# Masks moved into key rows, exps by bank, another merged order, one load of the spread queries, and a new start, in an eight-batch chain of four attentions

## The reference, cut to what matters

```
x = L0(x, ctx)        # 16 heads of 64, 256 positions, projections from x and ctx, layer norm
x = L1(ctx, x)        # 16 heads of 16, keys from [ctx, x] (256), key mask, MLP
x = L2(x, ctx)        # 16 heads of 16, 128 keys, key mask, MLP
x = L3(x, ctx)        # 16 heads of 8, 256 queries, 256 keys, key mask:
    attn = where(kv_mask, q @ k * scale, -inf); softmax
    mean = attn @ v; ex2 = attn @ (v * v); std = sqrt(relu(ex2 - mean**2))
    out  = (instance_norm(x) * std + mean) * mask
```

## Time and profile before

| | |
|---|---|
| median of three runs | 1008.47 us |
| the profiled execution, its own time | 1012.25 us |
| its span in the profile | 1010.5 us |
| TensorE busy (matmul) | 935.5 us, 93% of the span |
| VectorE busy | 559.5 us, 55% |
| ScalarE busy | 456.2 us, 45% |
| GpSimd busy | 292.4 us, 29% |
| DMA traffic | 86.54 MB, mean 86 GB/s |

### The profile page before, as it was taken

How to read it: one execution, slowest core, us unless ns; L and a number is a source line. 1 busy time by engine, 2 the same in 40 slices (tenths; PEclk the granted TensorE clock), 3 DMA queues, 4 the chain that set the end, 5 groups by cost and what they waited for, 6 DMA issues and landing times.

```text
span 1010.5 us, 21161 instructions
## 1 busy us (share of the span) xinstructions
PE 935.5 (93%) x8450; PEld 596.5 (59%) x8450; DVE 559.5 (55%) x890; ACT 456.2 (45%) x795; POOL 292.4 (29%) x402
## 2 busy tenths in 40 slices
PE   6989989999999998999999999999999999898995
PEld 5555764666647665567646666466665675455552
DVE  4344467445664557555675456644576546664554
ACT  2423444445444544445544454345544454442424
POOL 5230222334212432115322242124321243222401
PEclk9999999999999999999999999999999999999999
DMA  9500324113140132303241130401414031310220
GB/s 362 190 38 2 125 75 146 38 43 136 36 156 19 57 139 81 108 6 126 79 146 38 43 134 32 154 28 43 141 50 143 14 120 44 119 53 2 98 55 6
DMA packets 36728, 86.54 MB, mean 86 GB/s; under 512 B 8472, under 2 KB 26008, under 8 KB 28824
## 3 DMA queue, kind: packets, MB, share of 16 engines
q1 hardware_dynamic: 36632, 85.18, 24.5%
HBM read 77.24 MB, written 7.86 MB: 84 GB/s over the span
## 4 chain that ended last, share of the span: by engine, by line
PE 67%; DVE 12%; issue 6%; DMA 5%; ACT 5%; SPq 4%; POOL 1%; DVEq 0%; ACTq 0%; POOLq 0%
PE GP L1107 6%; PE GP L1118 6%; PE GP L660 6%; DVE nm L1592 5%; PE GP L662 5%; PE PV L821 4%; PE GP L1091 4%; PE PV L860 3%; PE GP L900 3%; PE SC L883 3%; PE PV L1031 3%; DMA Qx<-q_parts 2%; PE GP L667 2%; PE SC L1018 2%; PE SC L804 2%
## 5 line engine op out<-in xcount | busy, mean ns | idle before, releaser
L1592 DVE TENSOR_REDUCE nm<-MX 128x4 bf16<-128x1024 f32 (+1 forms) x168 | 206.4, 1229 | 125.3 <-PE MX L751 48.3
L1363 ACT ACTIVATE Pr<-SC 128x1024 f32<-128x1024 f32 x120 | 122.7, 1023 | 153.6 <-PE SC L883 76.9
L1966 POOL TENSOR_TENSOR Psum<-Pr 128x512 f32<-128x512 f32 x64 | 81.5, 1274 | 163.4 <-ACT Pr L1363 163.4
L660 PE MATMUL GP<-zP,W 128*128 128x128 f32 x512 | 106.3, 290 | 7.7 <-DMA W<-w 7.7
L662 PE MATMUL GP<-uP,W 128*128 128x128 f32 x512 | 99.7, 277 | 0.0
L660 PEld LDWEIGHTS GP<-zP,W 128*128 128x128 f32 x512 | 78.3, 193 | 29.0 <-issue 27.3
L1392 ACT ACTIVATE Pr<-SC,bcol 128x512 f32<-128x512 f32 x96 | 60.8, 685 | 51.3 <-PE SC L1018 50.7
L1934 POOL TENSOR_TENSOR stat<-stat,half 128x1 f32<-128x1 f32 x24 | 13.7, 570 | 224.4 <-DVE stat L1800 171.2
L662 PEld LDWEIGHTS GP<-uP,W 128*128 128x128 f32 x512 | 78.5, 194 | 0.0
L821 PE MATMUL PV<-Pr,V 128*64 128x256 f32 x512 | 70.8, 398 | 0.0
L1118 PE MATMUL GP<-WB,work 128*128 128x256 f32 x256 | 60.8, 386 | 6.5 <-DVE work L1731 6.4
(11 more groups left out here) (221 smaller groups left out, 1750.3 us busy)
## 6 DMA issues: line engine op xcount, KB each, us to landing
W<-w SPq DMA_DIRECT2D x20, 1024.0 KB, 5.3
WA<-w1a SPq DMA_DIRECT2D x8, 1024.0 KB, 7.2
WB<-w1b SPq DMA_DIRECT2D x8, 1024.0 KB, 9.5
WA<-w2a SPq DMA_DIRECT2D x8, 1024.0 KB, 4.8
WB<-w2b SPq DMA_DIRECT2D x8, 1024.0 KB, 7.0
Kx<-k_parts SPq DMA_DIRECT2D x24, 192.0 KB
Qx<-q_parts SPq DMA_DIRECT2D x24, 192.0 KB
scratch<-U SPq DMA_DIRECT2D x14, 256.0 KB, 2.0
```

The source lines that it names most:

```text
L660: pe.matmul(dst, W0[:, piece, 2 * s, at:at + P], zP[:, s * P:s * P + P], start=True, stop=False)
L1363: act.activation(Pr[:, n % 4:n % 4 + 2, :], SCP[:], ACT.Exp, scale=8.0 ** -0.5 if L else 0.125)\
L1592: dve.tensor_reduce(dst, MXP[:].rearrange("p i (a k) -> p i a k", a=a), AX_X, ALU.max, negate=True)\
L1966: pool.tensor_tensor(Psum[:, c % 4, :].rearrange("p (a l) -> p a l", l=D), two[:, :, 0:D], two[:, :, D:2 * D], ALU.add)\
```

## The change

It does this:

- **Mask in key rows.** The mask products (L725) are gone. Instead the two key tiles `K3b` get the mask row in rows that their own heads do not use (two VectorE operations per batch, after ScalarE has written the tiles), and the query tiles have 1.0 in one such row. There are now eight query tiles in place of four, each for one parity of groups; VectorE writes two of them (0 and 2), ScalarE the other six (all eight in the last batch). Four lie in free columns of `work`.
- **Exps by bank.** In L3 every batch takes one exp per bank, as only the last did.
- **Merged order.** The table `BOTH` is another one.
- **One load.** `Qx` rows 0 to 71 come by one DMA that reads `q_parts` three times.
- **W0 in halves.** Pieces 0 and 2 come in two halves each, in the order in which qp0, kp0, qp1 and kp1 need them.
- **Ten unread products** of 512 columns are issued by TensorE ahead of the projections, as soon as a tile of zeros is there.

```
-        (0, 4, [(0, 3, 2), ("rest", 0)], [(3, 0, 0)]),
-        (0, 5, [("den", 1), ("terms", 0), (0, 3, "T"), ("recip", 0, 0)], [(3, 0, 2)]),
-        (0, 6, [], [("recip", 0, 1), (3, 1, 0)]), (0, 7, [(3, 0, "T"), (3, 1, 2)], [("den", 2), (3, 2, 0)]),
-        (3, 0, [], [(3, 2, 2), ("den", 3), (3, 1, "T")]), (3, 1, [(0, 0, "B")], [(3, 2, "T")]),
...
+        (0, 4, [("rest", 0), (0, 3, 2)], [("terms", 0)]), (0, 5, [(0, 3, "T")], [(3, 0, 0), ("den", 1)]),
+        (0, 6, [("recip", 0, 0), (3, 0, 2)], [("recip", 0, 1), (3, 1, 0), (3, 0, "T")]),
+        (0, 7, [(3, 1, 2)], [("den", 2), (0, 0, "B"), ("den", 3)]),
+        (3, 0, [("recip", 1, 0), (3, 2, 0), (3, 1, "T")], []), (3, 1, [(3, 2, 2)], []),
...
-            for i in (0, 2, 4, 1, 3):
-                sp.dma_start(W0[:, i], w0[i]).then_inc(ld_w0[i] if i < 4 else ld_w0v, 16)
...
+            for i, h in ((0, 0), (2, 0), (0, 1), (2, 1)):
+                at = slice(D * h, D * h + D)
+                sp.dma_start(W0[:, i, :, at], w0[i][:, :, at]).then_inc(ld_w0[i][h], 16)
...
+            for i in (4, 1, 3):
+                sp.dma_start(W0[:, i], w0[i]).then_inc(ld_w0[i][0] if i < 4 else ld_w0v, 16)
...
-                for j in range(3):
-                    sp.dma_start(Qx[24 * j:24 * j + 24], q_parts).then_inc(ld_qx, 16)
+                sp.dma_start(Qx[0:72], q_parts.unsqueeze(0).to_broadcast([3, 3, 8, NH * D])).then_inc(ld_qx, 16)
...
-                    for i in range(2):
-                        half = slice(64 * i, 64 * i + 64)
-                        pe.matmul(M[i][:].rearrange("p (a k) -> p a k", k=D), sel[half, 0, :],
-                                  mrow[half, :].unsqueeze(1).to_broadcast([64, 2, D]), start=True, stop=False,
-                                  skip_group_check=True)
...
-                            mm = pe.matmul(M[i][:, s * D:s * D + D], Q3b[half, t, s * P:s * P + P],
-                                           K3b[half, g % 2, :], start=False, stop=True, skip_group_check=True)
+                            mm = pe.matmul(M[i][:, s * D:s * D + D], query3(v)[half, s * P:s * P + P],
+                                           K3b[half, g % 2, :], start=True, stop=True, skip_group_check=True)
...
+            pe.wait_ge(const_n, 1)
+            zeros = nm0[:].rearrange("p g s h -> p (g s h)")
+            for i in range(10):
+                pe.matmul(SC[0][:], zeros[:, 0:P], zeros, start=True, stop=True, skip_group_check=True)
...
+                    if L == 3:
+                        exps3(b, k)
...
+                    if b >= 0 and L == 0 and k in (4, 5):
+                        queries3(b, (1, 3, 4) if k == 4 else (6, 5, 7))
...
+                dve.wait_ge(s_K3v, b + 1)
+                for e in range(2):
+                    ins = dve.scalar_tensor_tensor(out=K3b[:, e, :], in0=b3row[:], scalar=hmask[:, 14 + e:15 + e],
+                                                   in1=K3b[:, e, :], op0=ALU.mult, op1=ALU.add)
+                ins.then_inc(s_K3b, 1)
```

More of the change, by code:

```diff
@@ L249, in build @@
         Q3b = sb("Q3b", [P, 4, D], BF16)
+        Q3c = work[:, 1536:2048].bitcast(BF16).rearrange("p (v l) -> p v l", l=D)
         V0 = sb("V0", [P, 2, 1024])
@@ L327, in row @@
             return rows[:, ROWS[name][0]:ROWS[name][0] + ROWS[name][1]]
-        ld_w0 = [sem(f"ld_w0_{i}") for i in range(4)]
+        ld_w0 = [[sem(f"ld_w0_{i}{h}") for h in ("a" if i % 2 else "ab")] for i in range(4)]
         ld_w0v = sem("ld_w0v")
@@ L511, in shifts, with query3 @@
             return (s_T3, 4 * b + g + 1) if L == 3 else (nmT_ready, SHIFTS.index((b, L, g)) + 1)
+        def query3(v):
+            return Q3b[:, v, :] if v < 4 else Q3c[:, v - 4, :]
         def turned3(b, g):
@@ L656, in project @@
                         piece, at = divmod((2 * i + c + (8 if name[0] == "k" else 0)) * P, 512)
-                        pe.wait_ge(ld_w0[piece], 16)
+                        pe.wait_ge(ld_w0[piece][0 if piece % 2 else at // D], 16)
                         for s in (s for s in range(2) if 2 * c + s in parts):
@@ L683, in ready_group @@
                         pe.wait_ge(s_Q3b, b + 1)
-                    elif g == 2:
-                        pe.wait_ge(s_Q3, b + 1)
+                    else:
+                        pe.wait_ge(s_Q3, 3 * b + g)
                     if g == 0:
@@ L1329, in highs3, with queries3, exps3 @@
                 act.activation(parts[:, 0, :], g[:, 0:D], ACT.Identity, bias=col("bq")).then_inc(s_Q3h, 1)
-            def queries3(b):
+            def queries3(b, which):
                 g = take(order_of(b), "q3")
                 act.wait_ge(s_Q3r, b + 1)
-                for t in range(0 if is_last(b) else 2, 4):
-                    ins = act.activation(Q3b[:, t, :], g[:, 0:D], ACT.Identity, scale=hmask[:, 4 + t:5 + t],
-                                         bias=col("bqm", t))
-                    if t == 1:
+                for v in which:
+                    ins = act.activation(query3(v), g[:, 0:D], ACT.Identity, scale=hmask[:, 4 + v:5 + v],
+                                         bias=col("bqm", v))
+                    if v == 2:
                         ins.then_inc(s_Q3b, 1)
-                ins.then_inc(s_Q3, 1)
-            def exps_last(b, k):
+                    elif v in (3, 6, 7):
+                        ins.then_inc(s_Q3, 1)
+            def exps3(b, k):
                 for j in range(2):
@@ L1354, in mixed @@
                     n = SC_AT[b + (L == 0), L, 2 * k]
-                    if is_last(b):
-                        exps_last(b, k)
+                    if L == 3:
+                        exps3(b, k)
                         if k == 4:
                             sums(b, 0)
+                        if k == 1 and b < B - 1:
+                            evacuate(b + 1, 3)
                         continue
@@ L1362, in mixed @@
                     pr_taken(act, n + 1, 1)
-                    act.activation(Pr[:, n % 4:n % 4 + 2, :], SCP[:], ACT.Exp, scale=8.0 ** -0.5 if L else 0.125)\
-                        .then_inc(p_ready, 2)
+                    act.activation(Pr[:, n % 4:n % 4 + 2, :], SCP[:], ACT.Exp, scale=0.125).then_inc(p_ready, 2)
                     if L == 0 and (k in (4, 6) or k == 2 and b < 0):
                         evacuate(b + 1, k // 2 - 1)
-                    if b >= 0 and L == 0 and k == 4:
-                        queries3(b)
+                    if b >= 0 and L == 0 and k in (4, 5):
+                        queries3(b, (1, 3, 4) if k == 4 else (6, 5, 7))
                     if b < 0:
@@ L1374, in mixed @@
                             cast(0, 2 + k // 2)
-                    if L == 3 and k == 4:
-                        sums(b, 0)
-                    if L == 3 and k == 1 and b < B - 1:
-                        evacuate(b + 1, 3)
             def mix_end(b):
@@ L1851, in body @@
                     dve.wait_ge(s_Q3h, b + 1)
-                    for t in range(2):
-                        ins = dve.tensor_scalar(Q3b[:, t, :], g[:, 0:D], col("bq"), hmask[:, 4 + t:5 + t],
-                                                ALU.add, ALU.mult)
+                    for v in (0, 2):
+                        ins = dve.tensor_scalar(query3(v), g[:, 0:D], hmask[:, 4 + v:5 + v], col("bqm", v),
+                                                ALU.mult, ALU.add)
                     ins.then_inc(s_Q3b, 1)
@@ L2090 @@
     bq = rows3(a["L3_xattn_bq"])
[L2091 removed]
+    bqm = np.zeros((8, P), bq.dtype)
     bk = rows3(a["L3_xattn_bk"])
@@ L2096 @@
             at = slice(32 * r + 8 * t, 32 * r + 8 * t + 8)
-            bqm[t, at], bkm[r % 2, at] = bq[at], bk[at]
+            bqm[2 * t + r % 2, at], bkm[r % 2, at] = bq[at], bk[at]
+            if t < 2:
+                bqm[[v for v in range(8) if v % 2 != r % 2 and (v < 2) == t], 32 * r + 8 * t] = 1.0
     w0 = np.stack([a["L0_xattn_" + n].T for n in ("Wqkv0", "Winj0", "Wqkv1", "Winj1")], axis=1)
```

49 lines of the change are left out of this document (25 added, 24 removed), and 2 rows, old and new, of the table TAKEN.

## The result

The changed kernel takes **1069.92 us** (median of four runs, 1066.80 to 1071.83), the kernel before beside it 1008.90 (1007.87 to 1010.12): a ratio of 1.060, interval 1.057 to 1.063. It is slower, as forecast, but by 61 us where 24.7 were forecast, and 1069.92 lies outside the range of 1013 to 1058. The profiled execution has a span of 1069.2 us, against 1010.5.

A forecast was written before the change was run, and what follows sets the result against it. TensorE, busy 93% of the span, was taken as the bound. Masks -12.3, order -3.5, query load +26.3, clock +6.5, last batch +5.4, start +2.3 gave +24.7 us on 1008.47: 1033.2 us, range 1013 to 1058.

The forecast's parts named there:

- masks, batches 0 to 6: TensorE's mask products removed: 56 pairs at 0.22 us each, -12.3 us.
- order: own gain, old waits and old drops of the clock gone: New table puts other work before waits for reductions: -3.5 us, bounds 0 and -6.0; old `Qx` waits and clock drops counted elsewhere.
- new waits for `Qx`, batches 0 to 6: TensorE waits before first exact scores: 3.7 us in three batches, 4.9 in four; 30.7 new less 4.4 old, +26.3 us.
- clock and what else follows a wait: Granted clock falls to about half behind a wait: 1.3 us a batch, +6.5 us for five more batches.
- last batch: Batch 7: load usable 5.0 us later, clock drop +1.3, four mask pairs saved -0.9; +5.4 us.
- start: Halves of `W0` in 1 KB rows lengthen the wait for value weights to nearly 4 us, clock falls: +2.3 us.
- the new load is usable 10.9 us after its issue: Single `Qx` load confined to three DMA engines like `Kx`: 9.6 us of data plus 1.3 to TensorE's start.
- TensorE's arrival: When TensorE reaches the first exact scores of L3: 283.7 in batch 1, 638.95 in batch 4.
- rival C: Load slower still, `WA` and `WB` following on its engines, 2 us more per load, clock falls twice: 1058 us, chance 0.08.
- Exps, query tiles and key rows: Extra ScalarE and VectorE work, costed at 0; failure would first show as TensorE waiting for `Q3b` ahead of L731.
- A: Single `Qx` load spreads as before, landing within about 7 us, no batch waits: -23.0 us, 985.5 us, chance 0.10.
- B: Most of the `Qx` wait is absorbed, TensorE late itself or later units without waits: +5.0, 1013.5 us, chance 0.05.

## Why the prediction was right in its sign and wrong in its size

The table sets the steps of the sum against what the spans and periods show. "Measured" in the seven batches goes in three steps: from the kernel before (824.7 us for the seven periods) to the version with three loads and masks again (817.7), to the version with three loads (806.1), to the changed kernel (875.3). The first step holds the order and also the exps, query tiles and key rows.

| step | forecast | measured |
|---|---|---|
| masks, batches 0 to 6 | -12.3 | -11.6 |
| order: own gain, old waits and old drops of the clock gone | -3.5 - 4.4 - 2.6 = -10.5 | -7.0 |
| new waits for `Qx`, batches 0 to 6 | +30.7 | +52.8 |
| clock and what else follows a wait | 7 x 1.3 = +9.1 | +16.4 |
| last batch | +5.4 | +5.0 |
| start | +2.3 | +3.0 |
| sum | +24.7 | +58.7 |

(52.8 is 59.8 less the 7.0 us of batch 7; 16.4 is 875.3 - 806.1 - 52.8. The last digits are rounded one by one.)

**The step that failed is "the new load is usable 10.9 us after its issue".** It was taken from `Kx`, which has the engines to itself, and from batch 7, where nothing follows the load. It is right for both situations: 10.7 us in batch 7, 10.1 to 10.7 with the weights held back. In batches 0 to 6, with 2 MB of weights and the inputs issued behind it, it is 14.4 to 15.1. The waits so became 52.8 instead of 30.7 us: 22.1 of the 34.0 us that were missing. The load by itself is worth more, 4.0 us in each of seven batches or 28; the rest is offset by two steps that erred the other way, TensorE's arrival (14.5 us after the query product, 14.0 forecast) and the issue in batches like 4 (7.2 us after it, where 10.2 less 1.7, 8.5, was forecast). The forecast knew of the difference: rival C named the weights, but priced it at 2 us for a load, with no row behind that figure, and with a chance of 0.08. C's time was the top of the range, 1058, and 1069.92 lies beyond it. No row of the kernel before showed a load of this form under other traffic, so the largest term of the sum had no bound from above, and a guess of 2 us stood for it.

What the load does on three engines is as read from the earlier trace rows. The Trainium skill's rule ("DMA: Bandwidth & Descriptors", Rules for kernel authors), that a leading zero-stride broadcast of c copies confines the DMA to at most c engines, agrees with the share of 0.17 to 0.18 in the two undisturbed cases. (The 3.4 us that the prediction took from the same page are by a formula that stands there for DMAs issued by GpSimd; this queue is SyncE's, and even the three loads with nothing behind them are usable only after 5.3 to 6.3 us.)

The same page says (Queues, rings and completion order) that on each engine descriptors are consumed in ring order. That is a rule on order and not on speed. By order alone, loads issued later would not delay an earlier one, and it would be usable after 10.5 us; the runs show 15.1 against 10.1 to 10.7. What changes is the rate: alone, each of the three engines moves 23 GB/s (67 GB/s at a share of 0.18), in batch 0 an engine moves 12 to 18 (201 and 319 GB/s at 1.08). An estimate from these: each of the three has 24 rows of 8 KB, which is 8.4 us at 23 GB/s and 11 to 16 us at 12 to 18; measured are 8 us of traffic alone and some 4 to 4.5 us more under the weights. Why an engine is so slow in that mixture is open. It is not the weights alone, which moved 393 to 434 GB/s once the three loads were over, and not the single load alone, which was fast in batch 7. The three loads are slow with nothing beside them (14 to 18 GB/s for an engine in batch 7), so many engines reading these 192 KB three times over, into the rows of `Qx`, may be enough; no run took this further.

**The clock** was right in kind and small in size: 1.3 us a batch, read from a drop of 3.5 us behind a wait of 1.64 us. Behind waits of 7.5 us the clock is at 1.2 GHz for 10.2 us, of which TensorE works some 7, and the cost is 16.4 / 7 = 2.3 us. With waits of 3 us (the weights held back) the seven periods are 838.9 us, 32.8 above the version with three loads, of which 21.0 are waits: 1.7 us a batch. These costs hold all that follows a wait; the clock's part in them is argued from the stretches, not measured alone. The cost grew with the wait, so an underpriced wait was paid twice.

**The masks** came at 0.21 us a pair where 0.22 was read, from starts and not from durations. **The order's** own 3.5 us did not show: the waits for reductions ahead of L731 were 6.0 us before, and are 7.2 with three loads and 4.2 in the changed kernel. What the order did give is what the forecast counted beside it, the old waits and drops, -7.0 measured for -7.0 forecast (the old order put back costs 7.9 us over the seven periods). The query load is issued 7.2 us after the query product in every one of these batches, where it was 8.6 to 10.2 before and 6.9 were forecast for batch 1. **Exps, query tiles and key rows** at 0: for the exps the run shows 1.0 us over the seven periods and 2.3 between the medians, near nothing but not settled; for the tiles and key rows it is argued only, from no wait of TensorE for `Q3b` among the large ones, since no run took them alone.

**The start**, +2.3, was +3.0, for the reasons given: the second half of the value weights is reached at 42.22 us behind a wait of 4.12 ("nearly 4"), and the clock is down for 3.4 us behind it. While the halves are read, from 5 to 9 us, the engines move 314 to 350 GB/s at a full share, with whole pieces, in the version that has them, 377 to 436. That the size was so near is partly luck: the seven profiles with this start reach the first query product 3.0 to 5.8 us later than before, and the changed kernel's is the earliest of them.

**The rivals.** A (the load spreads as before) gave 985.5 us. The load did not spread, but the version with three loads is the case that A describes: its span is 15.2 us below that of before (995.3 against 1010.5) where A's sum was -23.0. Most of the 7.8 us between are the order's 3.5, 1.8 at the start (155.26 - 151.12 = 4.1 instead of 2.3) and the wait of the last batch, which stayed. B (most of the wait is absorbed) fell: TensorE arrives 14.5 us after the query product, with and without the load, and waits it out. C had the mechanism, at half its size: 2 us a load where 4.0 were measured. Of the signs named beforehand, the share near 0.2 for 8 us in batch 7, the low clock behind the waits and the wait at 41 us came true; the waits of L883 were 7.1 to 7.8 us and not 3 to 6, 59.8 in all and not 35.

## What to carry to other kernels

Where a source is needed several times, try several loads that each read all of it before one (or several) whose outermost dimension repeats it: that line was worth 73 us here. A load's time measured with the queue to itself was a lower bound here; before it is put into a sum, look at what the same queue issues behind it, and if TensorE waits for the transfer, hold that traffic back or price the mixture. Take the clock's share together with the wait: each us of wait in this kernel cost 1.3 us (waits of 7.5), 1.6 (waits of 3) and 1.8 (the 1.64 of batch 4 before).
